# Where the input rows of a later round are turned in the expert loop of a decoder layer

## The chip, the cores and the metric

One core of one Trainium2 chip runs the whole layer as one program. The metric is the device time in microseconds (us): the median over several executions. Beside it stands one profiled execution, with its own time and its span from the first to the last instruction.

## The reference

A decoder layer over 8 x 256 tokens of width 512, in float32: linear attention, cross attention with 16 heads, and a mixture of 16 experts, each followed by a residual and a layer norm. The change is in the experts:

```python
top_val, top_idx = jax.lax.top_k(logits, 4)          # of 16 experts
gate_up = einsum('th,ehd->etd', x, gate_up_proj) + gate_up_proj_bias
gate = minimum(gate_up[..., ::2], 7);  up = clip(gate_up[..., 1::2], -7, 7)
glu = gate * sigmoid(gate * 1.702)
out = einsum('etd,edh->eth', (up + 1) * glu, down_proj) + down_proj_bias
out = (out * router_scores).sum over the experts
```

Only the four experts that a token chose have a score, so the kernel computes these alone.

## The kernel before

The layer runs in stages, one after the other: both attentions, a routing stage, the experts, and a last layer norm. The routing stage sorts the 8192 pairs of token and expert into tiles of 128 rows that belong to one expert each; there are at most 79 tiles, and with these inputs 76 are used. `experts` (from line 1599) works through them, one tile a round. Four rounds are unrolled (`U = 4`), and the loop of `loop` (line 1642) runs over these; at its end the sequencers branch back (line 1646). In round i, with j = i % 4, the engines do the following, each in its own written order.

- **TensorE** (`body`, line 1900): the gate products of tile i into `ps_g`; the turning (transposition, `transposes`, line 1860) of the intermediate rows `h` of tile i-1 into `ps_h` (`turn_h`); the up products of tile i into `ps_u`; the turning of the gathered input rows of tile i+2 into `ps_x` (`turn_x`, line 1865); the down products of tile i-1 into `ps_y` (`down`, line 1885). The products of one kind are 12 matmuls (line 1881): four pieces of the contraction, by three passes (`SPLITS`), since every float32 operand is kept as a high and a low half. Turning is 4 matmuls of 128x128 (line 1862).
- **ScalarE**: high half of the turned `h` (line 1747), the silu into `glu` (line 1789), high half of the turned input (line 1741, `x_hi`, which waits for the up products that read the same half of `xT4`), the weighted bias, and, in a round that starts a new expert, the high halves of the next expert's weights (line 1587).
- **VectorE**: biases and cuts in PSUM, low half of `hT` (line 1812), `h` itself (line 1846), the finished rows (line 1824), low half of the turned input (line 1808, `x_lo`).
- **GpSimd**: starts the gather of the input rows of tile i+3 (line 1687, an indirect DMA from `scratch_x` into one of four buffers `x_rows`), starts the scatter of the finished rows of tile i-2 (line 1697, added in DRAM), and makes the low halves of the next expert's weights (`split_lo`, line 1596): for each new expert 12 subtractions, six in the round that starts the expert and six in the round after it.
- **SyncE**: loads the weights of the next experts.

`turn_x` waits twice, in this order, before its first matmul:

```python
pe.wait_ge(gathered[j], 16 // U * (i - j) + 16)
if not is_at(i, 0):
    pe.wait_ge(xT_lo, i)
```

The first is the landing of the gather, the second the low half of the tile before it, after which `ps_x` is free. `down` and `body` begin with two loads of numbers from SBUF into registers of TensorE's sequencer (lines 1886 and 1887, 1901 and 1902: the tile's expert and its parity) and steps of register arithmetic, which give the weights' buffer and the values that the next waits compare with.

Of the kernel before, what the change touches and what calls it, by code (L numbers as in the profile page):

```python
# [1309 lines left out]
TILES = (TOK * K_TOP + E_ * (P - 1)) // P  # L1310
# [288 lines left out]
def experts(nc, A, S, x, G, W):  # L1599


    U = 4
    ROUNDS = TILES // U * U
    GATE, UP, DOWN = range(3)
    with ExitStack() as ctx:
# [35 lines left out]
        def loop(engine, body, end):  # L1641


            for j in range(U):
                body(j, j)
            with engine.Fori(1, TILES // U) as r:
                for j in range(U):
                    body(U * r + j, j)
            more = engine.value_load(G["active"][:, ROUNDS:ROUNDS + 1], min_val=0, max_val=1)
            with engine.If(more == 1):  # L1650
                for i in range(ROUNDS, TILES):
                    body(i, i % U)
                end(TILES - 1)
            with engine.If(more == 0):
                end(ROUNDS - 1)

        def is_at(i, n):
            return isinstance(i, int) and i == n
# [4 lines left out]
        def pick(table, i):  # L1663
            return table[:, i:i + 1] if isinstance(i, int) else table[:, bass.ds(i, 1)]
# [4 lines left out]
        @block.sync  # L1669
        def _(sp):  # L1670
            for e in range(2, E_):
                load_weights(sp, A, W, e)

                last = sp.value_load(G["last_tile"][:, e - 2:e - 1], min_val=0, max_val=TILES - 1)
                sp.wait_ge(y_ready, last + 1)
                load_biases(sp, A, W, e, e % 2)
# [181 lines left out]
        @block.tensor  # L1858
        def _(pe):
            def transposes(out, rows):  # L1860
                for c in range(KC):
                    mm = nc.tensor.transpose(out[:, c * P:(c + 1) * P], rows[:, c * P:(c + 1) * P], ident[:])  # L1862
                return mm

            def turn_x(i, j):
# [3 lines that stand above are left out]
                transposes(ps_x, x_rows[j]).then_inc(x_turned, 1)  # L1869

            def turn_h(i):
                pe.wait_ge(h_made, i + 1)
                if not is_at(i, 0):
                    pe.wait_ge(hT_lo, i)
                transposes(ps_h, h).then_inc(h_turned, 1)

            def products(out, left, par, k):

                passes = [(c, a, b) for c in range(KC) for a, b in SPLITS]
                for n, (c, a, b) in enumerate(passes):  # L1880
                    mm = nc.tensor.matmul(out[:], left[:, a, c], w[:, bass.ds(par, 1), k, b, c].squeeze(1),  # L1881
                                          start=(n == 0), stop=(n == len(passes) - 1))
                return mm

            def down(i):
                e = pe.value_load(pick(G["expert"], i), min_val=0, max_val=E_ - 1)
                par = pe.value_load(pick(G["parity"], i), min_val=0, max_val=1)
                pe.wait_ge(W["hi"], 3 * e + 3)
                pe.wait_ge(W["lo"], 3 * KC * e + 3 * KC)
                pe.wait_ge(hT_lo, i + 1)  # L1890
                if not is_at(i, 0):
                    pe.wait_ge(y_ready, i)
                products(ps_y, hT, par, DOWN).then_inc(y_made, 1)

            pe.wait_ge(W["small_loaded"][0], 16)
            pe.wait_ge(W["small_loaded"][1], 32)
            turn_x(0, 0)
            turn_x(1, 1)

            def body(i, j):  # L1900
                e = pe.value_load(pick(G["expert"], i), min_val=0, max_val=E_ - 1)
                par = pe.value_load(pick(G["parity"], i), min_val=0, max_val=1)

                pe.wait_ge(W["hi"], 3 * e + 2)
                pe.wait_ge(W["lo"], 3 * KC * e + 2 * KC)
                pe.wait_ge(W["small_loaded"][0], e // 2 * 16 + 16)
                pe.wait_ge(W["small_loaded"][1], (e + 1) // 2 * 16 + 16)
                pe.wait_ge(xT_lo, i + 1)
                if not is_at(i, 0):
                    pe.wait_ge(glu_made, i)  # L1910
                products(ps_g, xT[:, j % 2], par, GATE).then_inc(g_made, 1)
                if not is_at(i, 0):
                    turn_h(i - 1)
                    pe.wait_ge(h_made, i)
                products(ps_u, xT[:, j % 2], par, UP).then_inc(u_made, 1)
                if not (isinstance(i, int) and i >= TILES - 2):
                    turn_x(i + 2, (j + 2) % U)
                if not is_at(i, 0):
                    down(i - 1)

            def end(i):
                turn_h(i)
                down(i)

            loop(pe, body, end)


# [161 lines left out]
```

## Time and profile before

| | |
|---|---|
| median of 3 runs | 1657.0 us (1655.31 to 1657.11) |
| profiled execution: its time | 1659.04 us |
| profiled execution: its span | 1656.8 us |
| mean granted clock of TensorE | 0.948 of full speed |
| busy shares | TensorE 89%, weight loads 62%, VectorE 58%, ScalarE 43%, GpSimd 49% |
| first and last gate products | 892.7 us, 1602.6 us |
| last down products | 1616.1 us |

Shares are of the span. The profile names TensorE's matmuls PE, its weight loads PEld, and the sequencer that feeds both PEldq; GpSimd is POOL, VectorE DVE, ScalarE ACT. L1881 is line 1881 of the kernel. A merged row of the timeline starts where its first instruction starts; the end of a matmul is modelled, so lengths of work on TensorE are read here from one start to the next. The rounds are numbered from 0, by their gate products.

### The profile page before, as it was taken

How to read it: one execution, taken by the hardware profiler on the slowest of the kernel's cores; microseconds unless marked ns; L12 is line 12 of the kernel's file. 1: busy time of each engine (PE TensorE's matmuls, PEld its weight loads, DVE VectorE, ACT ScalarE, POOL GpSimd, SP SyncE). 2: the span in 40 equal slices, each digit the busy share in tenths (PEclk: the TensorE clock that was granted, in tenths of full speed). 3: DMA queues.
4: the chain of work that ended last, by engine and by line, in shares of the span. 5: the costliest groups of instructions: out<-in, count | busy, mean ns of one | idle time of the engine just before them, and what ended most of it. 6: DMA issues, size and time to landing. Idle time of an engine off the chain costs nothing. (4 is left out here: it accounts for less than half of the span.)

```text
span 1656.8 us, 28337 instructions
## 1 busy us (share of the span) xinstructions
PE 1473.6 (89%) x7422; PEld 1028.1 (62%) x7423; DVE 953.1 (58%) x1379; ACT 710.1 (43%) x1328; POOL 806.8 (49%) x650
## 2 busy tenths in 40 slices
PE   6988989779999999998346999999999999999990
PEld 5767767534444444442234788777777878877770
DVE  2333232667787777775195555555555555555555
ACT  4212111147777777777133244343443443434220
POOL 4424242423366546543332565666656576386222
PEclk9999999879999999999567999999999999999996
DMA  5101003343756574551171565665656576373326
GB/s 212 52 23 47 13 17 52 70 62 67 122 104 87 101 139 91 90 91 42 55 294 48 119 149 130 160 157 133 161 131 166 129 181 157 89 196 79 67 52 215
DMA packets 93712, 180.13 MB, mean 109 GB/s; under 512 B 17576, under 2 KB 20392, under 8 KB 93000
## 3 DMA queue, kind: packets, MB, share of 16 engines
q1 hardware_dynamic: 73944, 133.88, 32.0%
q0 software_dynamic: 18544, 44.84, 14.7%
q10 hardware_dynamic: 1152, 0.52, 0.2%
q8 instruction: 37, 0.61, 0.2%
q14 instruction: 35, 0.29, 0.1%
HBM read 115.55 MB, written 33.49 MB: 90 GB/s over the span
## 5 line engine op out<-in xcount | busy, mean ns | idle before, releaser
L823 DVE TENSOR_REDUCE stage<-ps_a 128x2 f32<-128x1024 f32 x256 | 300.7, 1218 | 95.9 <-PE ps_a L1042 95.3
L1596 POOL TENSOR_TENSOR we_split<-we_raw,we_split 128x512 f32 (+1 forms) x192 | 250.1, 1542 | 96.5 <-ACT we_split L1587 94.9
L635 ACT ACTIVATE probs<-ps_b 128x512 f32<-128x512 f32 x512 | 277.9, 595 | 44.4 <-PE ps_b L1057 42.0
L1881 PE MATMUL ps_y<-we_split,hT 128*128 x912 | 231.8, 403 | 4.2 <-DVE hT L1812 3.3
L1881 PE MATMUL ps_g<-we_split,xT 128*128 x912 | 230.2, 401 | 5.1 <-issue 4.2
L1881 PE MATMUL ps_u<-we_split,xT 128*128 x912 | 231.6, 403 | 0.0
L1881 PEld LDWEIGHTS ps_g<-we_split,xT 128*128 128x128 f32 x912 | 171.6, 190 | 53.4 <-issue 13.5
L1881 PEld LDWEIGHTS ps_y<-we_split,hT 128*128 128x128 f32 x912 | 166.2, 188 | 41.4 <-issue 6.6
L1881 PEld LDWEIGHTS ps_u<-we_split,xT 128*128 128x128 f32 x912 | 166.2, 189 | 34.8
L1697 POOL DMA_INDIRECT scratch_acc<-x_keep,to_rows x76 | 121.2, 1594 | 112.9 <-issue 52.9
L1747 ACT ACTIVATE hT<-ps_h 128x512 fp32r<-128x512 f32 x76 | 45.3, 596 | 296.7 <-PE ps_h L1862 253.8
L1057 PE MATMUL ps_b<-stack 55*128 55x512 f32 x512 | 132.1, 509 | 18.7 <-ACT probs L635 14.9
L1057 PEld LDWEIGHTS ps_b<-stack 55*128 55x128 f32 x512 | 51.3, 189 | 148.5 <-ACT probs L635 135.5
L1074 PE MATMUL ps_pv<-probs,v_aug 128*32 128x512 f32 x1024 | 142.3, 630 | 0.0
L1687 POOL DMA_INDIRECT x_rows<-scratch_x,from_rows x79 | 78.4, 993 | 111.5 <-ACT from_rows L1751 84.5
L1833 DVE TENSOR_TENSOR ps_g<-ps_g,we_bias 128x512 f32<-128x512 f32 x76 | 53.2, 700 | 116.0 <-PE ps_g L1881 84.5
L1824 DVE SCALAR_TENSOR_TENSOR x_keep<-ps_y,slot_weight_a,bw 128x512 f32<-128x512 f32 x76 | 57.1, 751 | 94.9 <-PE ps_y L1881 92.5
L1839 DVE TENSOR_TENSOR ps_u<-ps_u,we_bias 128x512 f32<-128x512 f32 x76 | 53.2, 699 | 88.4 <-PE ps_u L1881 88.4
L1741 ACT ACTIVATE xT<-ps_x 128x512 fp32r<-128x512 f32 x78 | 46.7, 598 | 119.3 <-PE ps_x L1862 117.8
L1042 PE MATMUL ps_a<-stack 53*128 53x512 f32 x512 | 88.6, 416 | 5.8 <-DVE stage L823 5.6
L1139 PE MATMUL ps_b<-stack,xT_split 128*128 128x512 f32 x384 | 92.4, 393 | 0.0
L1587 ACT ACTIVATE we_split<-we_raw 128x2048 f32 (+1 forms) x48 | 88.3, 1902 | 3.2 <-DMA we_raw<-in_w_expert 3.2
(214 smaller groups left out, 2123.2 us busy)
## 6 DMA issues: line engine op xcount, KB each, us to landing
we_raw<-in_w_expert SPq DMA_DIRECT2D x192, 256.0 KB
stack<-xT_raw SPq DMA_DIRECT2D x192, 128.0 KB, 5.3
we_bias<-in_b_expert SPq DMA_DIRECT2D x16, 768.0 KB, 4.2
stage<-in_w SPq DMA_DIRECT2D x5, 1024.0 KB, 5.0
xT_raw<-in_xT SPq DMA_DIRECT2D x4, 1024.0 KB, 6.3
x_tok<-in_x POOLq DMA_DIRECT2D x16, 256.0 KB, 3.1
late<-o_pair SPq DMA_DIRECT2D x128, 32.0 KB
late<-scratch_inv SPq DMA_DIRECT2D x16, 256.0 KB
```

What stands on the lines that cost most here:

```text
L635: nc.scalar.activation(probs[:, n % 3, h], src[:], ACT.Exp, scale=DH ** -0.5).then_inc(b_kept, 1)
L823: nc.vector.tensor_reduce(out[:, :, i, k % NC], ps_a[i][:], AX.X, ALU.max, negate=True).then_inc(a_kept[i], 1)
L1042: mm = nc.tensor.matmul(ps_a[i][:, e], q_stack[rows, slot, p, c * P:(c + 1) * P], k_stack[rows, slot, p, :], start=True, stop=True)
L1057: nc.tensor.matmul(out[:], k_stack[rows, slot, p, c * P:(c + 1) * P], q_stack[rows, slot, p, :], start=True, stop=True).then_inc(b_made, 1)
L1074: mm = nc.tensor.matmul(ps_pv[32 * h:32 * h + 32, :], v_aug[:, b % 2, c, 4 * g + h, :], probs[:, n % 3, h], start=(c == 0), stop=(c == NC ...
L1139: mm = nc.tensor.matmul(out[:], xT_split[:, xi, c, i * P:(i + 1) * P], w_split[w][:, wi, c, :], start=(n == 0), stop=(n == 3 * KC - 1))
L1587: nc.scalar.activation(dst, W["raw"][:, k], ACT.Copy).then_inc(W["hi"], 1)
L1596: nc.gpsimd.tensor_tensor(lo, W["raw"][:, k, c], hi, ALU.subtract).then_inc(W["lo"], 1)
L1687: pool.indirect_dma_start(x_rows[j][:], None, S["x2"], bass.IndirectOffsetOnAxis(from_rows[j][:], 0))\
L1697: pool.indirect_dma_start(S["acc"], bass.IndirectOffsetOnAxis(to_rows[j][:], 0), y[j], None, compute_op=ALU.add).then_inc(added, 16)
L1824: nc.vector.scalar_tensor_tensor(y[j], ps_y[:], pick(W["weight_a"], i), bw[:, j % 2], ALU.mult, ALU.add).then_inc(y_ready, 1)
L1881: mm = nc.tensor.matmul(out[:], left[:, a, c], w[:, bass.ds(par, 1), k, b, c].squeeze(1), start=(n == 0), stop=(n == len(passes) - 1))
```

## The change

In `body` of TensorE, `turn_x` moves from behind the up products to in front of them, directly behind `turn_h`. The wait for `h_made` stays directly in front of the up products. Nothing else is edited.

```diff
                 products(ps_g, xT[:, j % 2], par, GATE).then_inc(g_made, 1)
                 if not is_at(i, 0):
                     turn_h(i - 1)
+                if not (isinstance(i, int) and i >= TILES - 2):
+                    turn_x(i + 2, (j + 2) % U)
+                if not is_at(i, 0):
                     pe.wait_ge(h_made, i)
                 products(ps_u, xT[:, j % 2], par, UP).then_inc(u_made, 1)
-                if not (isinstance(i, int) and i >= TILES - 2):
-                    turn_x(i + 2, (j + 2) % U)
                 if not is_at(i, 0):
                     down(i - 1)
```

The order in which TensorE's instructions stand, in the last of the four unrolled rounds, in front of the up products. Of the kernel before (MATMUL stands for weight load and matmul; ISA is a step of the sequencer; `x_rows1` is a buffer of gathered rows, `gathered1` its landing, `xeT_lo` and `hT_lo` the low halves):

```order
L1881 MATMUL ps_g<-we_split,xT4 128x512 x2

L1862 MATMUL ps_h<-ident4,h 128x128 [waits hT_lo,h_made]

L1862 MATMUL ps_h<-ident4,h 128x128 x3

L1881 ISA [waits h_made]

L1881 MATMUL ps_u2<-we_split,xT4 128x512

L1881 ISA

L1881 MATMUL ps_u2<-we_split,xT4 128x512 x2

```

And of the change:

```order
L1881 MATMUL ps_g<-we_split,xT4 128x512 x2

L1862 MATMUL ps_h<-ident4,h 128x128 [waits hT_lo,h_made]

L1862 MATMUL ps_h<-ident4,h 128x128 x3

L1868 REGISTER_ALU [waits gathered1]

L1862 MATMUL ps_x<-ident4,x_rows1 128x128 [waits xeT_lo]

L1862 MATMUL ps_x<-ident4,x_rows1 128x128 x3

L1881 ISA [waits h_made]

L1881 MATMUL ps_u2<-we_split,xT4 128x512

L1881 ISA

L1881 MATMUL ps_u2<-we_split,xT4 128x512 x2

```

Between the turned `h` and the up products there are now the wait for `gathered1`, the wait for `xeT_lo` and four matmuls.

The same round in front of the down products, of the kernel before:

```order
L1881 ISA

L1881 MATMUL ps_u2<-we_split,xT4 128x512 x2

L1868 REGISTER_ALU [waits gathered1]

L1862 MATMUL ps_x<-ident4,x_rows1 128x128 [waits xeT_lo]

L1862 MATMUL ps_x<-ident4,x_rows1 128x128 x3

L1886 TENSOR_LOAD tile_expert

```

And of the change, on to the last wait ahead of the down products:

```order
L1881 ISA

L1881 MATMUL ps_u2<-we_split,xT4 128x512 x2

L1886 TENSOR_LOAD tile_expert

L1886 ISA x2

L1887 TENSOR_LOAD tile_parity

L1887 ISA x2

L1888 ISA

L1889 ISA [waits we_hi]

L1881 ISA [waits y_ready,hT_lo,we_lo]

```

The wait for the gather stood directly in front of the load of line 1886; now twelve products stand between them. On the other engines no instruction moves.

## Rows read from the trace of the kernel before

**Rows 1.** Stretch view, experts, TensorE only: us, busy (instructions), granted clock, DMA share, GB/s
```profile
940.00:1610.00 670.00, 665.28 (x3119) 1.00 0.56 133
```

**Rows 2.** Timeline of TensorE, an undisturbed round: start us, busy us, instructions merged
```profile
1215.34 2.98 PE L1881 MATMUL ps_g<-we_split,xT 128*128 x12
1218.16 0.60 PE L1862 MATMUL ps_h<-ident,h 128*128 128x128 f32 x4
1218.51 3.05 PE L1881 MATMUL ps_u<-we_split,xT 128*128 x12
1221.40 0.60 PE L1862 MATMUL ps_x<-ident,x_rows 128*128 128x128 f32 x4
1221.76 3.04 PE L1881 MATMUL ps_y<-we_split,hT 128*128 x12
1224.64 1.10 PE L1881 MATMUL ps_g<-we_split,xT 128*128 x4
```

**Rows 3.** Timeline of VectorE, same round: low half of next input tile
```profile
1216.41 0.68 DVE L1808 TENSOR_TENSOR xT<-ps_x,xT 128x512 fp32r<-128x512 f32 x1
```

**Rows 4.** Group view, 940 to 1610 us: busy us, mean ns, idle before
```profile
L1862 PE MATMUL ps_x<-ident,x_rows 128*128 128x128 f32 x284 | 42.5, 272 | 0.0
```

**Rows 5.** Timeline of GpSimd while one expert's weights are split
```profile
1186.04 1.00 POOL L1687 DMA_INDIRECT x_rows<-scratch_x,from_rows  x1 [0.15 <-issue]
...
1188.39 8.09 POOL L1596 TENSOR_TENSOR we_split<-we_raw,we_split 128x512 f32 x6
1196.64 1.00 POOL L1687 DMA_INDIRECT x_rows<-scratch_x,from_rows  x1 [0.16 <-issue]
```

**Rows 6.** TensorE's sequencer, round 32, by line: ns min/median/max, first to last start
```profile
L1868 PEldq ALU_OP  x1: 32/32/32, 1200.2 to 1200.2; - x1
...
L1886 PEldq TENSOR_LOAD <-tile_expert x1: 803/803/803, 1200.4 to 1200.4; - x1
```

**Rows 7.** Timeline of TensorE, round 32 and the next gate products
```profile
1199.17 3.05 PE L1881 MATMUL ps_u<-we_split,xT 128*128 x12
1202.05 0.60 PE L1862 MATMUL ps_x<-ident,x_rows 128*128 128x128 f32 x4
1202.76 3.07 PE L1881 MATMUL ps_y<-we_split,hT 128*128 x12
1205.94 3.08 PE L1881 MATMUL ps_g<-we_split,xT 128*128 x12
1208.86 0.60 PE L1862 MATMUL ps_h<-ident,h 128*128 128x128 f32 x4
```

**Rows 8.** Sequencer's load of line 1886: round 3, round 34 (undisturbed), round 67
```profile
L1886 PEldq TENSOR_LOAD <-tile_expert x1: 298/298/298, 925.8 to 925.8; - x1
...
L1886 PEldq TENSOR_LOAD <-tile_expert x1: 302/302/302, 1218.4 to 1218.4; - x1
...
L1886 PEldq TENSOR_LOAD <-tile_expert x1: 914/914/914, 1531.5 to 1531.5; - x1
```

**Rows 9.** Timeline of TensorE, round 3
```profile
924.64 3.05 PE L1881 MATMUL ps_u<-we_split,xT 128*128 x12
...
931.01 0.72 PE L1881 MATMUL ps_g<-we_split,xT 128*128 x2
```

**Rows 10.** Timeline of TensorE, round 67, the last round of a loop turn
```profile
1530.48 3.05 PE L1881 MATMUL ps_u<-we_split,xT 128*128 x12
...
1533.81 3.06 PE L1881 MATMUL ps_y<-we_split,hT 128*128 x12
1537.49 0.73 PE L1881 MATMUL ps_g<-we_split,xT 128*128 x2 [0.62 <-issue]
```

**Rows 11.** Sequencer's register steps of twelve down products, line 1881
```profile
L1881 PEldq FUSED_REGOPS  x8: 46/46/65, 1615.9 to 1616.9; - x8
```

**Rows 12.** Stretch view and timeline of TensorE, the first gate products
```profile
892.00:896.00 4.00, 3.31 (x8) 0.50 0.23 66
...
892.69 5.00 PE L1881 MATMUL ps_g<-we_split,xT 128*128 x12 [1.20 <-issue]
```

## The prediction

> **What bounds the kernel now.** I read the stretch view first, then the timeline of TensorE in single rounds, then the rows of its sequencer. In the experts TensorE is busy 665 of 670 us at the full clock [rows 1], so there every microsecond that TensorE loses is one of the kernel's, and nothing off TensorE matters unless it makes TensorE wait. An undisturbed round takes 9.30 us from one gate start to the next: 2.82 gate, 0.35 turning `h`, 2.89 up, 0.36 turning x, 2.88 down [rows 2].
>
> A few rounds take longer. GpSimd makes six low halves of weights behind each other (8.1 us) ahead of a gather; in round 32 it starts the gather that this round turns at 1196.64 [rows 5]. Up products begin at 1199.17 [rows 7], and the step that waits for the gather runs only at 1200.2 [rows 6]: the rows land 1.0 us after the up products began. The sequencer stands still until then, and behind the turning it still has two register loads and several steps before the first down product, 1200.4 to 1202.76 [rows 6, 7]. In an undisturbed round the load of line 1886 starts at 1218.4, 0.1 before the up products [rows 2, 8], and all this hides. In round 32 it does not: up start to the next gate start is 6.77 instead of 6.13 [rows 2, 7], and the gate products behind it take 2.92 for 2.82 [rows 2, 7], having no queued start. It lost 0.64 + 0.10 us.
>
> I went through all rounds in this way. The load of line 1886 starts more than 0.9 us behind the start of the up products in fifteen of them: round 3 (925.8 against 924.64), then one for each of 14 expert changes, the last of them round 67 (1531.5 against 1530.48) [rows 8, 9, 10]. Round 3 lost 0.24, round 67, in which the loop also branches back, 0.88 [rows 9, 10]. The fifteen together lost 10.3 us up to the next gate start and 1.4 behind it: **11.7 us, already paid before**.
>
> **The change, step by step.**
>
> 1. *The work itself.* Eight turning matmuls and 36 products stay. Four turning matmuls last 0.60 in all and one 0.272 [rows 2, 4], so they follow each other every 0.11. Two turnings back to back then take 4 x 0.11 + 0.35 = 0.79, and the down products, now directly behind the up products, should take the 2.82 that the gate products take behind the down products: 0.79 + 2.89 + 2.82 + 2.82 = 9.32, against 9.30. I cost it at 0. Its bounds: +0.02 x 74 = +1.5, and, if the second turning started 0.35 after the first as up products do, 9.23 a round, -5.2. I take the value from the matmuls' own step because the next turning is the same kind of instruction.
>
> 2. *The wait for the low half of the tile before.* It ends at 1216.41 + 0.68 = 1217.1, 1.4 us before TensorE wants to turn x, at 1218.5 [rows 2, 3]. The sequencer, which runs ahead, may stand at it for a moment, but with 12 gate products in the queue. Cost 0; were this cover gone, each round would pay.
>
> 3. *The wait for the gather.* It now stands in front of the up products. In a late round TensorE has nothing left when `h` is turned, and stops until the rows land. The stop is about the distance from the start of the up products, where x would now be turned, to the load of line 1886, since turning x can begin about when that load does: 1.2 in round 3, 1.2 in round 32, 1.0 in round 67 [rows 6 to 10]. Over the fifteen rounds these distances sum to 19.1; in three rounds an extra step stands between (as in round 32, 1200.2 to 1200.4 [rows 6]), so 18.8. Nothing hides it: +18.8. GpSimd's chain of splits does not wait for TensorE in between, so a loss in the round before only shortens this stop.
>
> 4. *What of the old loss comes back.* After the stop the sequencer issues 4 turnings and 12 up products; the register steps of twelve products take 1.0 [rows 11]. From the load of line 1886 to the first down product is 2.36, 0.50 of it because the load took 803 ns and not 302 [rows 6 to 8], so 1.9 usually. Issue of down is then 2.9 to 3.0 behind the start of turning x, and TensorE wants it at 0.35 + 2.89 = 3.24: in time. From down to gate the sequencer needs 3.18 [rows 7], so gate is ready at 6.15, wanted at 6.12: about nothing, 0.05 in ten rounds, 0.5. Where the loop branches back it needs 3.68 (1533.81 to 1537.49 [rows 10]): ready at 6.65, 0.5 late, and 0.1 behind that, in five rounds (15, 19, 23, 63, 67), 3.0. The rest of the 11.7 comes back: -11.7 + 0.5 + 3.0 = -8.2.
>
> 5. *Followers.* ScalarE's high half of x waits for the up products anyway; these now end where the turning ended, so it starts as before. `hT` is made while x and the up products run, as before. No queue on GpSimd or SyncE changes.
>
> Sum: 0 + 0 + 18.8 - 8.2 = **+10.6 us**, against the profiled execution's 1659.04 (span 1656.8). That execution lies 2.0 above the median of 1657.0; on the median I forecast 1657.0 + 10.5 = **1667.5**, the profiled one near 1669.5.
>
> Bounds of the sum. If all of the old loss comes back: 18.8 - 11.7 = +7.1, and with step 1's low end +1.9. If none of the lateness of down to gate comes back (only the 3.6 us between up and down of the 11.7 do): 18.8 - 3.6 = +15.2, with step 1's high end +16.7.
>
> The Trainium skill, page "DMA: Bandwidth & Descriptors", section "Anatomy of one DMA — SWDGE (gpsimd) path", gives a GpSimd DMA 2.0 us plus its bytes at 436 GB/s, an estimate of 2.6 for these 256 KB. The trace disagrees: 1196.64 to 1200.2 is 3.6 [rows 5, 6]. By the page the rows of round 32 would have landed at 1199.24, the stops would be about 0.2 each, and the sum 3 - 8.2 = -5; rival A gives the same outcome a mechanism of its own.
>
> **Rivals.**
>
> *A. Faster: the gather is not what holds the sequencer.* The loads of line 1886 in the late rounds are long themselves (803 and 914 ns against 302) and end at about the same distance from the up start, 2.1 and 1.9 [rows 6 to 8, 10]. If something else holds the sequencer there (the scatter, say) and the rows are there early, TensorE would hardly stop for x, and with the up products issued ahead of the loads the 11.7 would largely come back: 1657 - 8 = 1649. It decides from where the stops are below 0.5 us each. Against it: the step of line 1868, whose only wait is the gather, itself starts late, and the load follows it at once in round 3, where it took only 298 ns.
>
> *B. No change.* The stops are there but shorter, because the DMA's landing comes sooner, or turning back to back saves step 1's 5.2: 10.6 - 5.2 - 3 = +2, 1659.5.
>
> *C. Much slower: the clock.* Each of the fifteen stops leaves TensorE without work for over a microsecond. If the granted clock fell to 1.2 GHz behind each, one group of 12 products at that clock takes 4.8 to 5.0 for 2.98 [rows 2, 12], 2 us each: 1667.5 + 30 = 1697. Against it: through 670 us with these late rounds in them the granted clock is 1.00 [rows 1]. The Trainium skill, page "TensorE: Matmul & The Clock Gate", section "A second HAM failure mode: psum-queue depth-cycling", says that frequent short idling between groups of matmuls can make the clock go up and down; here the losses already there, 0.6 in a round, did not do it.
>
> *D. The wait of step 2 stops the sequencer in ordinary rounds.* It starves if the low half of x comes later than 1.4 us ahead. Some 0.1 us in 60 rounds gives +6, 1673.5. Against it: from 1217.1 until 1218.5 the sequencer has four turnings and the first up products to issue, which takes it some tenths.
>
> **How the numbers follow.** Main case, 1660.5 to 1674, 0.78, with D inside it at about 0.08; A 0.06; B 0.10; C and worse 0.06. A measurement of this kernel tells about 0.2%, 3.3 us, from no change. Faster by more: A, 0.06. Within: B without its upper edge and a piece of the main case's low end, 0.08. Slower: 0.86. The range runs from 1659.5, inside B, to 1674, the sum's high end, and leaves out A, C and the edges.
>
> **What would show it.** In the changed trace, in round 32 and its like, TensorE idle 1.0 to 1.4 us between turning `h` and turning x, about fifteen times, 18 to 19 us in all, the largest near 2 in round 63; behind them down directly at its time, and gate late only at the branch. Other rounds 9.30 as before, clock 1.00. The forecast is wrong if the idle time in front of `ps_x` is under 5 us, if ordinary rounds change by more than 0.03, or if the late rounds are other ones than before.

## The result and the profile after

| | before | changed |
|---|---|---|
| median, 8 runs each | 1657.9 us (1655.31 to 1666.86) | 1666.5 us (1660.56 to 1676.45) |
| ratio | | 1.006, 95% interval 1.0038 to 1.0082 |
| profiled execution, time | 1659.04 | 1666.02 |
| profiled execution, span | 1656.8 | 1663.9 |
| first gate products at | 892.7 | 888.0 |
| first to last gate start | 709.9 | 720.5 |
| last gate start to the end | 54.2 | 55.4 |

The change costs 8.6 us by the medians, and 6.3 to 13.6 by the interval of the ratio. In the two profiled executions the whole differs by 7.0, but the attention stages, which it does not touch, happened to end 4.7 us earlier in the second. From the first to the last gate start, 75 rounds, the difference is **10.6 us**. I use this stretch for profiles from here on, and medians for whole runs.

What TensorE waited for in the experts (the waits of TensorE, 895 to 1620 us: who for whom, us in total, times, longest):

```profile
PE ps_x L1862 <- DMA x_rows<-scratch_x,from_rows: 11.4, 14, 1.2
...
PE ps_y L1881 <- DVE hT L1812: 1.8, 1, 1.8
```

The first row is new: the gather's landing stops TensorE 14 times. The row counts from the modelled end of the turned `h`. Counted from one start to the next, as in the forecast, and less the 0.435 that lies between the two turnings in a round without a stop, the same 14 stops sum to 13.7 us. The trace also keeps each of the sixteen steps in which a gather reports its landing. In 13 of the 14 rounds the first turning of x starts 0.12 us behind the sixteenth step, in round 46 0.05 behind it. The stretch view, which stands against [rows 1]:

```profile
940.00:1610.00 670.00, 656.26 (x3076) 1.00 0.53 132
```

TensorE was idle for 13.7 of 670 us and not for 4.7, at the full clock still.

An ordinary round, 34, for [rows 2]:

```profile
1216.29 2.98 PE L1881 MATMUL ps_g<-we_split,xT 128*128 x12
1219.10 0.60 PE L1862 MATMUL ps_h<-ident,h 128*128 128x128 f32 x4
1219.54 0.60 PE L1862 MATMUL ps_x<-ident,x_rows 128*128 128x128 f32 x4
1219.89 3.05 PE L1881 MATMUL ps_u<-we_split,xT 128*128 x12
1222.79 2.98 PE L1881 MATMUL ps_y<-we_split,hT 128*128 x12
1225.60 0.63 PE L1881 MATMUL ps_g<-we_split,xT 128*128 x2
```

The second turning starts 0.44 behind the first, four steps of 0.11, the down products take 2.81, and the round 9.31 (9.30 before).

Round 32, for [rows 6, 7], on TensorE, in its sequencer, and on GpSimd:

```profile
1199.64 0.60 PE L1862 MATMUL ps_h<-ident,h 128*128 128x128 f32 x4
1200.73 0.65 PE L1862 MATMUL ps_x<-ident,x_rows 128*128 128x128 f32 x4 [0.49 <-DMA x_rows<-scratch_x,from_rows]
1201.14 3.05 PE L1881 MATMUL ps_u<-we_split,xT 128*128 x12
1204.03 2.97 PE L1881 MATMUL ps_y<-we_split,hT 128*128 x12
1206.87 1.43 PE L1881 MATMUL ps_g<-we_split,xT 128*128 x5
```

```profile
L1868 PEldq ALU_OP  x1: 32/32/32, 1200.6 to 1200.6; - x1
...
L1886 PEldq TENSOR_LOAD <-tile_expert x1: 308/308/308, 1201.9 to 1201.9; - x1
```

```profile
1197.07 1.00 POOL L1687 DMA_INDIRECT x_rows<-scratch_x,from_rows  x1 [0.16 <-issue]
```

The gather starts at 1197.07 and the step that waits for it runs at 1200.6, 3.5 us later (3.6 before). But `h` is turned from 1199.64, x could be from 1200.08, and is from 1200.73. Behind the stop the up products take 2.89 and the down products start right behind them: the load of line 1886, at 1201.9, is 2.1 ahead of them and took 308 ns. 803 ns was its length in the kernel before [rows 6]. The stop here is 0.65, less than elsewhere; round 31 had lost 0.3 already, which gave the gather more time.

Round 67, where the loop branches back, for [rows 10]:

```profile
1535.51 0.60 PE L1862 MATMUL ps_h<-ident,h 128*128 128x128 f32 x4
1536.75 0.65 PE L1862 MATMUL ps_x<-ident,x_rows 128*128 128x128 f32 x4 [0.64 <-DMA x_rows<-scratch_x,from_rows]
1537.15 3.05 PE L1881 MATMUL ps_u<-we_split,xT 128*128 x12
1540.05 2.97 PE L1881 MATMUL ps_y<-we_split,hT 128*128 x12
1543.22 0.96 PE L1881 MATMUL ps_g<-we_split,xT 128*128 x3 [0.21 <-issue]
```

A stop of 0.80, and 3.17 from down to gate where 2.81 is usual: the sequencer is 0.36 late.

### The profile page after: what moved, and what is told of

It is laid out like the page before. It is cut to its first block and busy times, and to the rows that moved or that the text cites. A ratio compares the mean times of both kernels' runs of the same rounds, so it can differ in the third digit from the quotient of the medians.

```text
span 1663.9 us, 28337 instructions
## 1 busy us (share of the span) xinstructions
PE 1470.6 (88%) x7422; PEld 1031.1 (62%) x7423; DVE 951.0 (57%) x1379; ACT 709.5 (43%) x1328; POOL 807.3 (49%) x650
## 3 DMA queue, kind: packets, MB, share of 16 engines
q0 software_dynamic: 18544, 44.84, 13.6%
## 5 line engine op out<-in xcount | busy, mean ns | idle before, releaser
L1881 PEld LDWEIGHTS ps_y<-we_split,hT 128*128 128x128 f32 x912 | 173.3, 190 | 46.2 <-issue 4.0
```

## The experiments

**Theory 1**, that of the forecast: rows land late at 14 expert changes, and TensorE stops for all of it that is not behind other work; the sequencer's steps behind the wait are a second, smaller loss. **The rival**: turning x in front of the up products costs by itself, in every round. Single rivals stand in the expectations.

### The changed kernel once more

> The changed kernel unaltered, once more, beside the kernel before on the same chip. Theory 1 (TensorE stops for late gathers at the 14 expert changes): +8.6 us again within 3, and in the profile 13 to 19 us of idle time in front of ps_x in some 14 rounds, in the same rounds as the first time. Rival (the difference lies in ordinary rounds or in the single fall of the clock near 905 us): the idle time moves to other rounds or the fall of the clock is gone and the difference with it.

Measured: 1667.15 us against 1658.05 (16 runs of the kernel before), ratio 1.0054 (1.0037 to 1.0072). First to last gate start 719.9; 14 stops again, in the same rounds, 13.8 us. The clock fell again behind the stop of round 1, near 910 us. So the stops are the program's and not an execution's.

### Gathers one round earlier, in both kernels

```diff
 # ScalarE (aim_from) and GpSimd (gather), in front of the loop and in body
-            for j in range(3):
+            for j in range(4):
                 gather(j, j)
...
-                if not (isinstance(i, int) and i >= TILES - 3):
-                    gather(i + 3, (j + 3) % U)
+                if not (isinstance(i, int) and i >= TILES - 4):
+                    gather(i + 4, j)
```

(The table of tokens gets one more column, since the last round now gathers a tile that nobody uses, and GpSimd's last wait counts this gather too.)

> The changed kernel with every gather started one round earlier on GpSimd (four tiles ahead instead of three; no further buffer is needed). Theory 1: no gather is late any more, the idle time in front of ps_x in the rounds behind the second is below 1 us, the down products start directly behind the up products everywhere, and the experts take about 18 us less than in the changed kernel (first to last gate start 720.5 to about 702); the kernel is about 10 us faster than the kernel before, near 1647. Rival (turning x in front of the up products costs by itself, through the wait for the low half or the sequencer): rounds stay long and the kernel stays at or above the kernel before.

> The kernel before with every gather started one round earlier, the same edit as in after_g4. Theory 1: the 11.7 us that late gathers cost it go, near 1646, and with early gathers the place of turn_x makes no difference: equal to after_g4 within 2 us. Rival (the place of turn_x costs by itself): after_g4 is slower than this kernel by as much as the changed kernel is slower than the kernel before, 8 us.

Measured, and measured once more with the same two kernels:

> after_g4 unaltered, once more, beside before_g4_b on one chip: the first pair gave medians 3.5 us apart with the sign against the profiles. By the stretch of the experts in the profiles (700.3 against 698.8) turning x in front costs 1.5 us with early gathers; theory 1 and its step 1 expect 0 to +2 us against before_g4_b. Rival (early turning gains by itself): 3 us faster again, with a stretch below 699.

> before_g4 unaltered, once more: about 1647 to 1650, the stretch of the experts at 698.8 within 0.5, 8 to 11 us faster than the kernel before.

| | median | ratio to the kernel before | first to last gate start |
|---|---|---|---|
| changed, gathers early | 1645.96 | 0.9925 (0.9903 to 0.9946) | 700.3 |
| again | 1649.7 | 0.9946 (0.9927 to 0.9966) | 701.2 |
| before, gathers early | 1649.45 | 0.9946 (0.9927 to 0.9964) | 698.8 |
| again | 1646.66 | 0.994 (0.9917 to 0.9963) | 699.2 |

The changed kernel with early gathers, the waits of TensorE in the experts, all of them, and round 32:

```profile
PE ps_y L1882 <- DVE hT L1813: 3.4, 2, 1.8
PE ps_h L1863 <- issue: 1.7, 1, 1.7
```

```profile
1194.40 0.60 PE L1863 MATMUL ps_h<-ident,h 128*128 128x128 f32 x4
1194.83 0.60 PE L1863 MATMUL ps_x<-ident,x_rows 128*128 128x128 f32 x4
1195.19 3.04 PE L1882 MATMUL ps_u<-we_split,xT 128*128 x12
1198.07 2.28 PE L1882 MATMUL ps_y<-we_split,hT 128*128 x9
```

No row for the landing is left. x is turned 0.43 behind `h`, up products start 0.36 behind that, down 2.88 behind them. Twenty microseconds of the changed kernel are gone, and 11 of the kernel before, so the kernel before had paid 11 us for the same late gathers without ever stopping at `ps_x`. Between the two places of `turn_x` 1.5 and 2.1 us remain in the stretch, 1.4 and 1.6 of it from round 2 on, about 0.02 a round; the medians of whole runs, once 3.5 us one way and once 3.0 the other, cannot tell these apart. The rival, that the place itself costs 8 us, falls. Both versions are faster than both kernels.

### Gathers 1.9 us later

```diff
+                if not below(i, 2):
+                    scatter(i - 2, (j - 2) % U)
                 if not (isinstance(i, int) and i >= TILES - 3):
                     gather(i + 3, (j + 3) % U)
-                if not below(i, 2):
-                    scatter(i - 2, (j - 2) % U)
```

> The changed kernel with each gather started behind the scatter of its round instead of in front of it, 1.9 us later where GpSimd is busy with the weights. Theory 1: every microsecond of lateness is one of TensorE's: each of the 14 pairs of late rounds costs 1.9 us more, +26 us against the changed kernel, and the first round of each pair now stops too. Rival (the stop is not the gather's landing but follows the scatter or the register loads): the scatter, now earlier, makes it no worse, under +8 us.

Measured: 1712.2 us, ratio 1.0323 (1.0293 to 1.0352), +45 against the changed kernel, first to last gate start 766.1. Both theories missed the size. The waits of TensorE, then round 27 and its clock in the stretch view:

```profile
PE ps_x L1862 <- DMA x_rows<-scratch_x,from_rows: 40.1, 21, 2.8
```

```profile
1167.23 0.60 PE L1862 MATMUL ps_h<-ident,h 128*128 128x128 f32 x4
1169.92 0.65 PE L1862 MATMUL ps_x<-ident,x_rows 128*128 128x128 f32 x4 [2.09 <-DMA x_rows<-scratch_x,from_rows]
1170.33 4.59 PE L1881 MATMUL ps_u<-we_split,xT 128*128 x12
1174.75 2.97 PE L1881 MATMUL ps_y<-we_split,hT 128*128 x12
```

```profile
1170.00:1174.00 4.00, 4.00 (x14) 0.65 0.68 205
```

From start to start the stops grew from 13.7 us in 14 rounds to 43.8 in 22, 30 where 26 was expected. The gathers themselves also took longer: the median from start to landing is 4.2 us here and 3.5 in the changed kernel. That may be where the extra 4 come from; it was not tried by itself. Of the other 15.5 us in the stretch nearly all, 14, is the clock. Turning `h` to turning x takes 2.69 here, and behind it the up products take 4.42 for 2.89: for a part of 1170 to 1174 the granted clock was 1.2 GHz. It fell in nine rounds, each of them behind a stop of over 2 us (2.1 to 3.0), and cost about 1.5 us each. It did not fall behind the other five stops of over 2 us (round 14: 2.2, round 48: 2.6), and in the changed kernel it fell only behind the 1.8 us stop of round 1, behind none of the 14 of 0.65 to 1.35. The second theory of the expectation, that the stop follows the scatter and not the gather, falls.

### The two loads in front of the wait

```diff
                 products(ps_u, xT[:, j % 2], par, UP).then_inc(u_made, 1)
+                loaded = of_tile(i - 1) if not is_at(i, 0) else None
                 if not (isinstance(i, int) and i >= TILES - 2):
                     turn_x(i + 2, (j + 2) % U)
                 if not is_at(i, 0):
-                    down(i - 1)
+                    down(i - 1, loaded)
```

(`of_tile` holds the loads of lines 1886 and 1887.)

> The kernel before with the two register loads of the down products (tile's expert, parity) in front of turn_x's wait, behind the up products; the place of turn_x as in the kernel before. Theory 1 (the loss of the kernel before is the sequencer's 1.9 us of loads and steps behind the late landing): the down products start on time in the 15 late rounds, and most of the 11.7 us go: first to last gate start 709.9 to about 699 to 701, the kernel near 1648. Rival (the loads themselves are slow there because the scatter or the landing disturbs them, whatever stands around them): they are slow in front of the wait too and little is gained, under 4 us.

Measured: 1648.1 us, ratio 0.9943 (0.9926 to 0.996), first to last gate start 699.6. Round 32, in the sequencer and on TensorE:

```profile
L1887 PEldq TENSOR_LOAD <-tile_parity x1: 306/306/306, 1193.0 to 1193.0; - x1
...
L1868 PEldq ALU_OP  x1: 32/32/32, 1194.0 to 1194.0; - x1
```

```profile
1192.91 3.05 PE L1881 MATMUL ps_u<-we_split,xT 128*128 x12
1195.79 0.60 PE L1862 MATMUL ps_x<-ident,x_rows 128*128 128x128 f32 x4
1196.15 3.04 PE L1881 MATMUL ps_y<-we_split,hT 128*128 x12
1199.03 0.64 PE L1881 MATMUL ps_g<-we_split,xT 128*128 x2
```

The rows land as late as ever: the step of line 1868 runs at 1194.0, 1.1 behind the start of the up products. But the second load has run at 1193.0, only a few steps are left behind the wait, and the down products start at 1196.15, 3.24 behind the up start, on time. The stretch is 10.4 us shorter with gathers as late as before, and 11.3 from round 2 on, which is all of the old loss: round 0 happened to take 0.8 more. So a late landing costs the kernel before what the sequencer still had to do behind the wait. The long loads (803 ns) were part of that path; in front of the wait, in these rounds, they take 0.3. They did not vanish: 28 loads take over 0.4 us in either kernel, but here none of them stands in one of the 14 late rounds.

### x turned in the middle of the up products

```diff
                 for n, (c, a, b) in enumerate(passes):
+                    if n == 6 and halfway:
+                        halfway()
                     mm = nc.tensor.matmul(...)
```

> The kernel before with turn_x between the sixth and the seventh of the twelve up products. Theory 1 (TensorE stops only for rows that land later than the place where they are turned; behind the wait the sequencer still needs 1.9 us and 0.5 us for six more products before the first down product): rows that land 1.0 to 1.4 us behind the up start are 0.1 to 0.5 early here, so hardly any idle time in front of ps_x, under 1 us in all; but the down products start about 0.3 to 0.5 later than in the kernel before, and the kernel is 3 to 7 us slower than the kernel before, between the two. Rival (only TensorE's stop counts, not what the sequencer has behind the wait): equal to the kernel before within 1 us in the stretch of the experts.

Measured: 1661.7 us, ratio 1.0023 (1.0005 to 1.0041); first to last gate start 712.0, but 0.9 of the 2.1 more lies in round 0, so 1.2. Round 15, one of the late ones:

```profile
1041.92 1.65 PE L1883 MATMUL ps_u<-we_split,xT 128*128 x6
1043.41 0.60 PE L1862 MATMUL ps_x<-ident,x_rows 128*128 128x128 f32 x4
1043.77 1.64 PE L1883 MATMUL ps_u<-we_split,xT 128*128 x6
1045.54 3.07 PE L1883 MATMUL ps_y<-we_split,hT 128*128 x12
1049.21 0.97 PE L1883 MATMUL ps_g<-we_split,xT 128*128 x3 [0.61 <-issue]
```

x is turned 1.49 behind the up start, at its time, and nowhere in the run is there a stop in front of it. The down products start 3.62 behind the up start, where [rows 10] and [rows 7] have 3.33 and 3.59 and an undisturbed round 3.24. That is 0.4 late, as expected, but the kernel before already lost most of this (3.48 in its own round 15), so the stretch gives +1.2 and not 3 to 7: I had added the new lateness to the old one where it takes its place. The rival of equality within 1 is not far off by the stretch. Whole runs do not decide it: the interval of their ratio allows 0.8 to 6.8 us. The order of the three places, late turning 709.9, halfway 712.0, early 720.2, holds.

### The two loads in front of the wait, in the changed kernel

```diff
+                loaded = of_tile(i - 1) if not is_at(i, 0) else None
                 if not (isinstance(i, int) and i >= TILES - 2):
                     turn_x(i + 2, (j + 2) % U)
                 if not is_at(i, 0):
                     pe.wait_ge(h_made, i)
                 products(ps_u, xT[:, j % 2], par, UP).then_inc(u_made, 1)
                 if not is_at(i, 0):
-                    down(i - 1)
+                    down(i - 1, loaded)
```

> The changed kernel with the two register loads of the down products in front of turn_x's wait (the same edit as in before_hoist; here this place is in front of the up products). Theory 1 (13.7 us of stops in front of ps_x are the landing alone and stay; only what is late behind them, the gate products where the loop branches back and in the rounds before a stop, is the sequencer's): the stops sum to 13 to 16 us, the 4 us lost between down and gate go, and the first to last gate start is 715 to 718, against 720.2 in the two profiles of the changed kernel; 2 to 4 us faster than it, still slower than the kernel before. Rival (the sequencer's work makes the stops too): the stops shrink as the loss did in before_hoist, and the stretch falls below 710.

Measured: 1664.2 us, ratio 1.0035 (1.0018 to 1.0053), first to last gate start 717.1. The landing's row of TensorE's waits:

```profile
PE ps_x L1862 <- DMA x_rows<-scratch_x,from_rows: 12.7, 14, 1.1
```

From start to start the stops are 15.2 us, in 15 rounds, since round 3 stops for 0.25 here; the time lost between down and gate fell from 4.1 to 0.3. The edit that gave the kernel before 10.4 us gives the changed one 3: what the sequencer has behind the wait matters little when TensorE itself stands in front of it. The stops grew by 1.5, since in the rounds before a stop no time is lost any more, which had shortened them.

### Both edits in the kernel before

> The kernel before with both edits, gathers one round earlier and the two register loads in front of turn_x's wait. Theory 1 (each edit alone takes away the same loss, the one its cause, the other its effect): no gain over either, first to last gate start 698.5 to 699.5, median 1645 to 1649. Rival (they take away different losses): a stretch below 695, or some 10 us faster than either.

Measured: 1646.6 us, ratio 0.9945 (0.9924 to 0.9966), first to last gate start 698.4: no gain over either. They take away one and the same loss.

## Why the prediction was right

The forecast was 1667.5 us, +10.5; measured were 1666.5 and +8.6, and in the stretch of the experts +10.6. The mechanism and its sign hold, and so do its rounds but for round 3. That the stretch comes out at just the sum's 10.6 is luck: the stops were put 5.1 too high, what comes back 2.8 too high, and 2.2 us of work and clock were put at nothing; these errors cancel.

1. *The work itself, 0.* An ordinary round went from 9.295 to 9.31, as the matmuls' own step said; over 73 rounds +1.1, and with early gathers 1.4 and 1.6. The other bound, that the second turning starts 0.35 behind the first (-5.2), was wrong.
2. *The wait for the low half, 0.* Right: no such stop, and rival D did not occur.
3. *The stops, +18.8.* They measured 13.7, in 14 rounds and not 15. Five things shortened them. Round 3 does not stop. Its lateness in the kernel before was of another kind: fifteen of the gather's sixteen steps had landed 3.65 us behind its start, at 924.4 and so ahead of the up products (924.64 [rows 9]), and the last only after 5.0. In the changed kernel the sixteenth came after 3.5, and the gather started 1.4 earlier against the gate products, since rounds 1 and 2 were longer (below); either is enough, so 1.2 us of the forecast rested on one late step of sixteen. (The forecast says against rival A that the step of line 1868 starts late in round 3. It ran at 923.8, 2.0 ahead of the load; what the load followed at once was the last step of the landing, at 925.79.) x would now be turned 0.08 later than the up products used to start, because the turning of `h` comes right before it: 14 x 0.08 = 1.1. I measured to the load of line 1886, 0.12 behind the step of line 1868 as a rule, while turning x starts 0.09 behind that step: 0.4 in all. From their start to the step of line 1868 the gathers took 0.1 less each than in the kernel before (13 of these rounds compared), 1.4 in all, over half of it in rounds 63 and 15; why is open. And the rounds just before a stop lose 0.3 to 0.4 themselves in several cases (27, 31, 59), and that comes off the stop, as the run with hoisted loads showed by 1.5. This last I had named but priced at zero.
4. *What comes back, -8.2.* Not counting stops, the rounds from 2 on lost 12.0 us before and 6.6 after, -5.4. The down products are in time behind every stop, as worked out. What I missed is that the rounds just before a stop, in which the rows land about when `h` is turned, also leave the sequencer little time, and are late at gate. At the branch the lateness was 0.36 to 0.96, forecast 0.5.
5. *Not in the sum, +1.1.* In round 1, where TensorE waits 1.8 us for `hT` in both kernels, the clock fell in the changed one:

```profile
904.00:909.00 5.00, 4.53 (x14) 0.69 0.69 209
...
904.47 4.28 PE L1881 MATMUL ps_y<-we_split,hT 128*128 x12 [1.79 <-DVE hT L1812]
908.55 0.99 PE L1881 MATMUL ps_g<-we_split,xT 128*128 x2
```

Round 1 of the kernel before:

```profile
909.14 3.07 PE L1881 MATMUL ps_y<-we_split,hT 128*128 x12 [1.75 <-DVE hT L1812]
912.10 1.19 PE L1881 MATMUL ps_g<-we_split,xT 128*128 x4
```

Down to gate takes 4.08 us, for 2.96 in round 1 of the kernel before, with the clock at 0.69 of full on average, where before the wait was as long and the clock stayed. Another 0.3, in the gate products of round 2, is in term 4. The clock fell there in three of the six profiles of kernels that turn x in front of the up products, and in none of the six of kernels that turn it in the middle or behind. That the change brings it on is not shown: the stop is the same 1.8 us, and in two other profiles with x turned early the clock stayed behind it (in the third, with hoisted loads, this stop is only 0.9).

So +1.1 + 13.7 - 5.4 + 1.1 = 10.5, and 0.1 in round 0.

Rival A (the gather is not what holds the sequencer) had a true part: the loads were long in the late rounds. But the sequencer stood at the wait for the gather, whose landings end the stops. From the start of the gather to the step that waits for it these 14 rounds have 3.3 to 4.4 us, in both kernels. The Trainium skill, page "DMA: Bandwidth & Descriptors", section "Anatomy of one DMA — SWDGE (gpsimd) path", gives 2.0 us and the bytes at 436 GB/s, an estimate of 2.6 for these 256 KB; the trace disagrees. Rival B had one small true piece, the gathers that took 0.1 less. Rival C, the clock, has the right mechanism and the wrong place: behind the 14 stops it never fell, and with stops of over 2 us it did. The Trainium skill, page "TensorE: Matmul & The Clock Gate", section "A second HAM failure mode: psum-queue depth-cycling", says that frequent short idling between groups of matmuls can make the clock go up and down. These runs show both: 14 stops of 0.65 to 1.35 us without a fall, and nine falls behind 14 stops of over 2 us.

## What to carry to other kernels

A transfer's lateness costs by what stands behind its wait: in front of long work it costs TensorE all of itself, behind it only the sequencer's path to the next matmul, which loads and register steps make long and which can be moved ahead of the wait. Before an operation is moved forward, compare the landing of its input with the new place in the worst rounds, here 14 of 76, and not in the typical one: in round 34 of the changed kernel the rows had landed 9.7 us before they were turned. Best is to remove the lateness: the fourth buffer was free a round earlier than it was used, and starting the gather there gave some 0.6% where the move lost as much.

## What was not expected of the hardware

- A register load by TensorE's sequencer, 0.30 us elsewhere, took 0.5 to 0.99 us in the late rounds of the kernel before and in the rounds just before them. Over all twelve profiles it follows the scatter, and not the round: every one of the 238 loads in the experts that began 2.0 to 2.9 us behind the start of a scatter on GpSimd took 0.4 to 1.0 us, and 207 of them ended 3.2 to 3.4 behind it, whenever they began; of those that began less than 1.9 or more than 2.9 behind only two did. That the scatter holds them is inferred from these times; no run leaves the scatter out.
- The granted clock fell behind idle stretches of over 2 us in nine rounds of one kernel and not in five others of the same length; each fall cost about 1.5 us.
- In eight of the twelve profiles the sixteenth step of one gather, the one that GpSimd starts next to its first scatter (that of round 3 in the kernel before), landed 0.8 to 1.6 us behind its fifteenth; in the other four 0.01 to 0.11 behind. Why was not tried.
